# One ScalarE copy moved two places later in the fourth step of the narrow cross-attention loop

## The reference

```
q = layernorm(x) @ Wq + bq        # 128 -> 128
k = ctx @ Wk + bk;  v = ctx @ Wv + bv
s = clip(q k^T over 8 features, scaled, minus its row maximum)
p = softmax(s) over the 64 keys of the same batch row
x = x + tanh(g) * ((p v) @ Wo + bo)
```

## Time and profile before

| what | value |
|---|---|
| median of 3 runs | 3090.51 us (3088.66 to 3094.82) |
| the profiled execution's own time | 3090.51 us |
| its span in the profile | 3088.5 us |
| PE busy over the span | 2907.3 us (94%) |
| DVE busy | 2219.8 us (72%) |
| ACT busy | 1577.6 us (51%) |
| POOL busy | 1181.7 us (38%) |
| layer 4 in the span | about 1345 to 1646 us |

### The profile page before, as it was taken

One profiled execution on the slowest core, in us unless ns is written; L12 is line 12 of the kernel. 1 busy time (PEld: TensorE's weight loads), 2 busy tenths in 40 slices (PEclk: granted clock), 3 DMA queues, 4 the chain that ended last, 5 costly groups with the idle time before them and its releaser, 6 DMA issues. The chain is left out here.

```text
span 3088.5 us, 89570 instructions
## 1 busy us (share of the span) xinstructions
PE 2907.3 (94%) x34642; PEld 2271.6 (74%) x34642; DVE 2219.8 (72%) x5750; ACT 1577.6 (51%) x2906; POOL 1181.7 (38%) x1274
## 2 busy tenths in 40 slices
PE   7999799999998999869997999999998999999978
PEld 6888545555556888747776888888886888888854
DVE  6777566666654666668887777788766788888756
ACT  6777312111113777537774333333335777777756
POOL 6677200000003777554540000000004677777753
PEclk9999899999998999979998999999998999999999
DMA  5000165666551000011111333333330000000001
GB/s 158 19 10 8 62 195 175 184 181 186 168 168 35 12 10 10 2 53 26 26 25 57 111 103 104 105 96 97 106 111 16 12 10 10 8 10 10 10 1 55
DMA packets 110871, 212.03 MB, mean 69 GB/s; under 512 B 18737, under 2 KB 30449, under 8 KB 110194
## 3 DMA queue, kind: packets, MB, share of 16 engines
q1 hardware_dynamic: 110194, 209.03, 22.5%
q10 hardware_dynamic: 512, 0.92, 0.1%
HBM read 198.34 MB, written 5.77 MB: 66 GB/s over the span
## 5 line engine op out<-in xcount | busy, mean ns | idle before, releaser
L341 PE MATMUL ps<-parts 128*128 128x512 f32 (+3 forms) x1568 | 624.2, 398 | 32.9 <-DVE parts L955 18.8
L342 PE MATMUL ps<-parts 128*128 128x512 f32 (+3 forms) x1568 | 565.2, 360 | 0.0
L343 PE MATMUL ps<-parts 128*128 128x512 f32 (+3 forms) x1568 | 563.2, 359 | 0.0
L311 POOL TENSOR_TENSOR rstd<-mv,eps 128x4 f32<-128x4 f32 x112 | 23.2, 207 | 1205.1 <-DVE mv L294 1204.9
L1878 ACT ACTIVATE work<-ps 128x512 f32<-128x512 f32 x272 | 162.3, 597 | 442.1 <-PE ps L343 442.0
L341 PEld LDWEIGHTS ps<-parts 128*128 128x128 f32 (+2 forms) x1568 | 299.7, 191 | 104.7 <-ACT work L790 26.2
L537 POOL TENSOR_TENSOR work<-work 128x512 f32<-128x512 f32 x256 | 267.5, 1045 | 276.7 <-DVE work L925 276.7
L343 PEld LDWEIGHTS ps<-parts 128*128 128x128 f32 (+2 forms) x1568 | 298.7, 191 | 46.2
L342 PEld LDWEIGHTS ps<-parts 128*128 128x128 f32 (+2 forms) x1568 | 301.3, 192 | 20.2
L1843 PEld LDWEIGHTS ps<-early,work 128*128 128x128 f32 x2176 | 281.4, 192 | 18.9 <-DVE pause L1932 0.3
L1843 PE MATMUL ps<-early,work 128*128 128x128 f32 x2176 | 287.9, 276 | 0.1
(11 more groups left out here) (284 smaller groups left out, 6083.7 us busy)
## 6 DMA issues: line engine op xcount, KB each, us to landing
work<-gate_rows SPq DMA_DIRECT2D x128, 512.0 KB, 5.5
work<-expert_rows SPq DMA_DIRECT2D x512, 128.0 KB, 2.9
work<-gate_rows SPq DMA_DIRECT2D x128, 256.0 KB, 6.6
work<-in_ctxT SPq DMA_DIRECT2D x72, 192.0 KB, 2.4
out<-x SPq DMA_DIRECT2D x16, 256.0 KB, 2.3
work<-work SPq DMA_DIRECT2D x224, 16.0 KB
work<-work SPq DMA_DIRECT2D x16, 128.0 KB, 2.3
early<-in_l0f_w SPq DMA_DIRECT2D x1, 1536.0 KB
```

The lines of the kernel that those rows point to most:

```text
L341: T.matmul(out, lh, rh, start=True, stop=False)
L342: T.matmul(out, lh, rl, start=False, stop=False)
L343: return T.matmul(out, ll, rh, start=False, stop=True)
```

## The change

In the ACT list of layer 4, in step 3 of every unit that has a next one, the copy of the first half of the next unit's values is written behind `take_out` and the first `take_probs`, where it stood ahead of both. Nothing is added or removed.

```
                     for t in range(TG):
                         un, n = Unit(it, u, 1), it * 8 + (4 * u + t)
                         end = last and u == 1
-                        if t == 3 and not end:
-                            take_values(un.next(), 0)
                         if not (isinstance(n, int) and n < 2):
                             take_out(n - 2, t)
                         take_probs(n, t, 0)
+                        if t == 3 and not end:
+                            take_values(un.next(), 0)
                         if t == 0 and not end:
                             take_turned(un.next())
```

## The result

The changed kernel takes 3113.26 us (median of 5 runs) against 3094.82 us for the kernel before in the same comparison. The ratio is 1.0062, with a 95% interval of 1.0048 to 1.0077; a second comparison gave 1.0063 (1.0050 to 1.0077). One of the five runs took 7164 us and stands outside the ratio. The change makes the kernel slower by some 19 us. The prediction had 9 us, 3099.7 us and a range to 3107: the sign was right, the size half of the measured.

What follows compares the result with a forecast made beforehand. PE, 96% busy in layer 4's body, was taken as the bound. 15 x 1.26 = 18.9 us lost less 14 x 0.69 = 9.7 given back is +9.2 on 3090.5: 3099.7 us, 8-in-10 range 3093 to 3107.

Steps and rivals of the forecast that it cites:

- The head of the ACT step holds nobody up: ACT, step 3: L1341 and the first L1337 wait for PE anyway, so moving the copy gains them nothing.
- The stall of 1.26 us, 15 times: PE, step 3: L1194 starts 1.26 us later, waiting for the moved copy; 15 times, 18.9 us lost.
- the three links: Step 3: transposes to their ACT copy 0.64 us, values copy 0.50 later taking 0.60, PE following 0.05 after.
- The slack of step 0 is given back: PE, step 0: L1387 comes after POOL's L1142, so the wait for L1389 goes; 14 x 0.69 = 9.7 us back.
- The rival that kept the slack, 3109.4 us: PE, step 0: still waits 0.73 us as before, so the whole 18.9 us stays; chance 0.09.
- The rival in which PE fills the stall: PE, step 3: takes L1235's matmuls ahead of waiting L1194; net -5.8 us, 3084.7 us; chance 0.04.
- No change: Rival: each unit's delay stays within the 0.69 us slack of step 0; 3090.5 us; chance 0.19.
- The clock: Layer 4: PE's granted clock read as 1.00 throughout, no term inside the layer; 2 us either way for the next layer.

Runs made afterwards that it cites:

- half of the move: Against the kernel before, the values copy in step 3 placed behind take_out but ahead of take_probs; 3093.4 us, ratio 1.0001.
- the one with the stall filled: Changed kernel with eleven unused transposes on PE ahead of its step 3 wait for the copy; 3098.8 us, ratio 1.0023 to the kernel before.
- with the bias moved: Changed kernel with POOL's bias addition L1142 moved from step 3 to step 1, behind the clamp; 3110.5 us, ratio 1.0058 to the kernel before.

## Why the prediction was off by half

*The head of the ACT step holds nobody up:* right. L1341 and L1337 start where PE lets them, as before.

*The stall of 1.26 us, 15 times:* right. It measured 1.24, by the three links as predicted, and PE's waits for it sum to 17.6 us (18 predicted).

*The slack of step 0 is given back:* right. The wait for L1389 is gone, L1387's mean is 275 ns (about 260 predicted), and the layer with PE kept busy is 8.7 us longer where the sum had 9.2. The rival that kept the slack, 3109.4 us, is nearest to the measured time and yet wrong: PE no longer waits in step 0, and moving L1142 in the changed kernel gained none of the 10 us of the layer that it would have to. That nearness is a chance; a time alone would have taken it for shown.

*The rival in which PE fills the stall:* its order was wrong, as the waits show, and so was its price of -5.8 us. When PE was made to do it, the time was that of before. I had let L1387 go short in a case where PE is too little late for that.

*No change:* the reasoning held, as a delay within the slack is hidden (half of the move), but 1.24 us a unit is not within 0.69.

*The clock:* this is the step that failed. The prediction read the granted clock as "1.00 throughout" and carried it over to a program in which PE stands idle for twice as long in one piece. The sum has no term for the clock inside the layer; it was put at nothing without a reason, and only the next layer had 2 us. What happened in its place are seven stretches of 3.4 us at 1.2 GHz inside the layer. From the changed kernel to the one with the stall filled the layer shortens from 312.7 to 302.3 us, which is 10.4 us or 1.5 us for each. That is somewhat less than half of a stretch's 3.4 us. The sum comes out: 8.7 and 10.4 are the 19.1 us of the layer.

The kernel before has one wait of 0.6 us in a unit and no fall. The changed one has one of 1.2 us and a fall in about every second unit; 0.96 us brought none in the profiled execution. The trace of before showed inside the layer only where the clock held, and nothing in it bounded what a longer idle would do; so the prediction needed a rival for it. The Trainium skill names such a case: its page on TensorE (TensorE: Matmul & The Clock Gate, section "A second HAM failure mode: psum-queue depth-cycling") tells of another kernel in which short idles between groups of matmuls were frequent enough that the clock went back and forth. The runs here agree as far as idles of 1.17 us, once in 18.0 us, brought seven falls in 15 stalls, and once in 36 us two in seven.

Open is when exactly a stall brings a fall. The time line has two steps alike in PE's busy time with and without one; in both profiled executions of the changed kernel it was every second stall, and with the bias moved it was none before 1528 us, then three times every second one, and none at the last stall. Across the 26 executions of the changed kernel that took about 3.11 ms, the mean clock of the whole program lies between 0.968 and 0.974 and the span between 3119.4 and 3100.7 us, the lower clock with the longer span (correlation -0.88). The kernel before has nearly the same relation (-0.80 in 27 executions) and no fall in this layer in its profile, so this speaks of the clock in the whole program and doesn't show how many falls layer 4 had.

## What to carry to other kernels

A copy that frees a shared buffer belongs where its reader will next need the buffer, and not behind copies that themselves wait for that reader: count the new chain from the reader's last instruction to the copy's end. A delay is then first set against the slack that the bounding engine has in the same period, and half of the move here cost nothing that could be measured (1.0001), for that reason. And where PE is the bound, price a new idle of PE twice: its length, and the clock that may fall after it; work put into the idle, even useless work, shows which of the two it is.

## What was not expected of the hardware

PE's clock fell after a single idle of 1.2 us in a stretch where PE was busy for 2.22 of 3.40 us, in a layer where it was busy for 93% of the time (230.54 of 247.00 us). Eleven useless transposes a unit, put into that idle, made the changed kernel 14 us faster. And a DVE operation of 0.17 us, held for 0.8 us beside one POOL operation, cost the kernel before 9 us in this layer, which moving that POOL operation by two steps won back.
